# z with time steps on partitions, y gated as it leaves PSUM, q's sums on TensorE, and gates broadcast by DMA

## The chip, the cores and the metric

The kernel runs on one core of a Trainium2 chip. The metric is the device time of one execution in microseconds (us). The engines are TensorE (PE), VectorE (DVE), ScalarE (ACT), GpSimd (POOL) and SyncE (SP, which issues every DMA here). Each executes its own list of instructions in order, and they meet only in semaphores.

## The reference, cut to what matters

Eight sequences of 256 steps and 256 channels pass through a Mamba block and then a linear attention block.

```python
xz = xn @ in_proj_w.T;  x_in, z = split(xz)            # 512 channels each
u  = silu(causal_conv4(x_in) + conv_b)
dt, B, C from x_proj(u)                                # N = 16 states
h  = h * exp(dt * A) + (dt * u) * B                    # scan over 256 steps
y  = sum_n(h * C) + u * D_param
y  = y * silu(z)                                       # gated
x  = x + gate[b] * (y @ out_proj_w.T)                  # gate: one row of 256 per batch
q  = softmax over the 32 channels of a head;  k = softmax over the 256 steps
att = k.T @ v (per head);  y = q @ att
x  = x + (silu(ln(y) * (1 + scale) + shift) @ W_out + b_out)
```

## The kernel before, in words

**Units.** A batch's scan has 512 channels (4 chunks `dc` of 128 partitions) by 16 states. It is cut into 16 units `g`, each of one chunk and 4 states: 128 partitions by 4 x 256 steps. Eight batches give 128 units. For each, ACT computes the decays into one of two PSUM buffers `ring` (`decays`, L504), POOL the inputs into one of five buffers `hs` (`inputs_of`, L383), DVE scans (L635) and multiplies by C (L639), and PE adds the four products into the bank `YT`, by transposing matmuls against the identity (L940), which leaves steps on partitions. `decays(g)` waits until the multiplication of unit g-2 has released its ring buffer.

**Slots.** All other work of a batch is a step with a fixed slot, written out by hand: at loop index g every engine first does its part of unit g and then the steps whose slot, plus 16 times a batch, equals g (`due`). Since slots count modulo 16, three batches are interleaved: the projections of the next (slots -24 to -1), the scan (0 to 15), and what follows the scan (16 to 41). Below, "position" is the slot modulo 16.

**Around y.** After a chunk's four units DVE copies `YT` to `yt` (`copy_sums`, L646, at positions 4, 8, 12 and 0). At slot 18 (position 2) PE waits for the four copies and transposes them back into the banks PZ and PY (`transpose_back`, L956), behind `in_proj_2` of a later batch, which waits for DVE's convolution taps. At slot 19 (position 3) DVE multiplies the two banks by `zs` = silu(z), channels on partitions (`gate_y`, L654), into `yg`, the input of `out_proj` (PE, slot 19). Then come `gate_x` (DVE, slot 21), `residual` (POOL, slot 24) and the attention block.

**Around z.** `in_proj` (PE, L901) has four calls; calls 2 and 3 give z, and ACT copies or gates their result (L451, L455, L457).

**Around q and k.** DVE takes the maxima of q over heads and of k over steps, subtracts q's, and negates k's with a `tensor_scalar` on 128 x 2 elements (`max_qk`, position 11, L673 to L682). ACT exponentiates (`exp_qk`, position 14). DVE sums q's exponentials over heads and takes both reciprocals (`sums_qk`, position 13, L686 to L692). PE multiplies k by v (`k_times_v`, L1016, slot 31) when ACT has copied both transposes; DVE scales the result into `att` (`head_blocks`, L699, position 0); PE multiplies q by it (L1024); DVE divides by q's sums (`normalize_q`, L706, position 1).

**Gates.** During the first batch PE multiplies rows of the identity by `gate8` to spread each batch's gate row over 128 partitions, in two halves (`setup_gates`, L865), and DVE copies the banks PY and PZ to `gate` (L787, g = 11 and 14).

**ACT at position 7** does `silus`: two table loads around the silus of z, u and, from the fourth on, of the attention block's output.

Of the kernel before, what the change touches and what calls it, by code (L numbers as in the profile page):

```python
# [19 lines left out]
P = 128  # L20
# [41 lines left out]
def build(nc, a, out):  # L62
    ctx = ExitStack()
    with ctx:
# [28 lines left out]
        gate = sb("gate", [P, NB, D])  # L93
# [12 lines left out]
        zs = sb("zs", [P, 2, DC, T])  # L106
# [8 lines left out]
        yt = sb("yt", [P, DC, TC, P])  # L115
# [7 lines left out]
        qmax, qsum, rq = sb("qmax", [P, TC, HEADS]), sb("qsum", [P, TC, HEADS]), sb("rq", [P, TC, HEADS])  # L123
# [9 lines left out]
        fin = sb("fin", [P, TC, D])  # L133
        bc_dram = nc.dram_tensor("bc_rows", (2, 2 * N, T), F32, kind="Internal").ap()
# [32 lines left out]
        s_gate_mm = sem("gate_mm")  # L167
        s_gate_ready = sem("gate_ready")
# [30 lines left out]
        s_yt_ready = sem("yt_ready")  # L199
# [22 lines left out]
        s_qrec_step = sem("qrec_step")  # L222
# [21 lines left out]
        bc_loaded = [[sem(f"bc_loaded{i}_{q}") for q in range(UPC)] for i in range(2)]  # L244
        s_out_stored = sem("out_stored")
# [5 lines left out]
        def xz_bank(b, h):  # L251

            return (PX, PY, PZ, ring[:, 0, 0:2, :])[h] if b == 0 else PX

# [7 lines left out]
        def _(sp):  # L262
# [6 lines left out]
            def broadcast_bc(b):  # L269
# [142 lines left out]
        def _(act):  # L412
# [34 lines left out]
            def copy_z(b):  # L447
                act.wait_ge(s_xz_mm, 4 * b + 3)
                if b >= 2:
                    act.wait_ge(s_yg_ready, 2 * (b - 1))  # L450
                nc.scalar.activation(zs[:, b % 2, 0:2, :], xz_bank(b, 2)[:, :, :], ACT.Copy).then_inc(s_z_ready, 1)  # L451

            def silu_z(b):
                act.wait_ge(s_z_ready, 3 * b + 1)
                nc.scalar.activation(zs[:, b % 2, 0:2, :], zs[:, b % 2, 0:2, :], ACT.Silu).then_inc(s_z_ready, 1)  # L455
                act.wait_ge(s_xz_mm, 4 * b + 4)
                nc.scalar.activation(zs[:, b % 2, 2:4, :], xz_bank(b, 3)[:, :, :], ACT.Silu).then_inc(s_z_ready, 1)  # L457
# [49 lines left out]

            def normalize1(b):
# [18 lines left out]
            def exp_qk(b):  # L527
                act.wait_ge(s_qsub_ready, b + 1)
                nc.scalar.activation(qe[:, :, :], qe[:, :, :], ACT.Exp).then_inc(s_qe_ready, 1)
                act.wait_ge(s_kmax_ready, 2 * (b + 1))  # L530
# [50 lines left out]
            for g in range(FIRST, LAST):  # L581
# [6 lines left out]
                for slot, step in ((-17, normalize0), (-16, modulated), (-15, conv_last_tap_0), (-14, conv_last_tap_1),  # L588
                                   (-11, copy_z), (-6, copy_xdbl), (-5, softplus_parts_0), (-3, softplus_parts_1),
                                   (25, normalize1), (26, norm1), (30, exp_qk), (31, mask_v), (32, copy_qT),  # L590
# [9 lines left out]
        def _(dve):  # L600
# [41 lines left out]
            def copy_sums(b, dc):  # L642
# [467 lines left out]
```

## Time and profile before

| | us |
|---|---|
| median of 3 runs | 667.79 |
| lowest, highest | 666.66, 671.83 |
| profiled execution | 668.15 |
| its span, first to last instruction | 666.3 |
| DVE busy | 589.3 |
| PE busy, PE weight loads busy | 452.1, 376.6 |
| ACT busy | 405.9 |
| POOL busy | 389.4 |

The profile records one execution; 1.85 us of its time lie outside the span. Busy time counts an instruction from start to end, and consecutive DVE instructions can overlap by some tens of ns, so distances between starts are the better measure of what an instruction costs. The mean granted TensorE clock was 0.843 of full speed.

### The profile page before, as it was taken

Reading aid. Unit: us, or ns where it says so; the run is one execution under the profiler, and the core shown is the slowest. Engines: PE = TensorE matmul, PEld = TensorE weight load, DVE = VectorE, ACT = ScalarE, POOL = GpSimd, SP = SyncE. Lnnn points to the kernel's source line nnn. Section 1 sums busy time; section 2 is a strip of 40 time slices with the busy share of each in tenths; the row PEclk is TensorE's granted clock in tenths of the full one; section 3 lists DMA queues with packets and bytes.
Section 4 is the critical chain, followed back from the end, with each engine's and each line's share of the span. In section 5 each row is a group of like instructions: output and inputs, shape, how many; then the busy total and the mean of one; then the engine's idle time right before and its main releaser. Section 6 shows DMA issues by size and latency. Waiting matters only on the chain.

```text
span 666.3 us, 7102 instructions
## 1 busy us (share of the span) xinstructions
PE 452.1 (68%) x2352; PEld 376.6 (57%) x2352; DVE 589.3 (88%) x618; ACT 405.9 (61%) x874; POOL 389.4 (58%) x292
## 2 busy tenths in 40 slices
PE   3848687678566756778567856776666956775764
PEld 3637566566465645666456745665665756654642
DVE  4809999999999999999999999999999999999321
ACT  2374756558655868387755866487737774754232
POOL 4066759547855786557845694657746696661100
PEclk9978876898689789889689778989789966877886
DMA  7273042002400070005200160007000240000000
GB/s 214 70 248 122 1 162 92 1 16 78 178 1 0 19 268 1 0 17 179 92 0 13 50 226 1 0 16 260 12 0 1 82 190 0 1 16 1 0 16 17
DMA packets 19870, 44.31 MB, mean 67 GB/s; under 512 B 2348, under 2 KB 11060, under 8 KB 19829
## 3 DMA queue, kind: packets, MB, share of 16 engines
q1 hardware_dynamic: 19832, 43.84, 18.9%
q8 instruction: 19, 0.31, 0.2%
q14 instruction: 19, 0.16, 0.1%
HBM read 41.48 MB, written 2.36 MB: 66 GB/s over the span
## 4 chain that ended last, share of the span: by engine, by line
DVE 58%; issue 14%; PE 11%; ACT 9%; POOL 6%; DMA 1%; DVEq 0%; SPq 0%; ACTq 0%; POOLq 0%
DVE ring L635 33%; DVE hs L639 8%; DVE conv L625 5%; POOL hs L383 4%; PE YT L940 3%; ACT ring L504 3%; PE PY L983 2%; DVE st L605 2%; DVE yt L646 2%; DVE kmax L682 2%; PE PX L901 1%; ACT L455 1%; PE PX L836 1%; PE PY L1024 1%; ACT L578 1%
## 5 line engine op out<-in xcount | busy, mean ns | idle before, releaser
L383 POOL TENSOR_TENSOR hs<-dtu,BC 128x1024 f32<-128x1024 f32 x128 | 299.7, 2358 | 107.8 <-PE YT L940 107.7
L635 DVE TENSOR_TENSOR_SCAN ring<-ring,hs 128x1024 f32<-128x1024 f32 x128 | 292.1, 2282 | 20.2 <-POOL hs L383 16.2
L504 ACT ACTIVATE ring<-dt,Aneg 128x256 f32<-128x256 f32 x512 | 213.2, 464 | 149.2 <-DVE hs L639 149.1
L940 PE MATMUL YT<-ident,hs 128*128 128x128 f32 x1024 | 160.0, 312 | 51.5 <-DVE hs L639 51.4
L940 PEld LDWEIGHTS YT<-ident,hs 128*128 128x128 f32 x1024 | 139.9, 163 | 67.6 <-DVE hs L639 62.5
L639 DVE TENSOR_TENSOR hs<-ring,BC 128x1024 f32<-128x1024 f32 x128 | 156.8, 1225 | 4.4
L901 PE MATMUL PX<-xnT,win 128*128 128x256 f32 x232 | 67.0, 439 | 27.2 <-ACT xnT L435 11.2
L901 PEld LDWEIGHTS PX<-xnT,win 128*128 128x128 f32 x232 | 48.8, 222 | 39.9 <-ACT xnT L435 13.6
L983 PE MATMUL PY<-wqkvo,xT 128*128 128x256 f32 x192 | 63.3, 489 | 0.0
L983 PEld LDWEIGHTS PY<-wqkvo,xT 128*128 128x128 f32 x192 | 49.5, 258 | 10.2
L362 POOL TENSOR_TENSOR dt<-dt,conv 128x512 f32<-128x512 f32 x16 | 20.3, 1271 | 53.0 <-ACT conv L484 53.0
L935 PE MATMUL YT<-ident,uD 128*128 128x128 f32 x64 | 16.4, 347 | 46.3 <-DVE yt L646 44.7
L444 ACT ACTIVATE conv<-PX,par 128x256 f32<-128x256 f32 x30 | 15.2, 557 | 47.2 <-PE PX L901 47.2
L935 PEld LDWEIGHTS YT<-ident,uD 128*128 128x128 f32 x64 | 9.4, 176 | 50.1 <-DVE hs L639 49.7
L625 DVE SCALAR_TENSOR_TENSOR conv<-PX,par,conv 128x255 f32<-128x255 f32 (+2 forms) x90 | 36.3, 473 | 0.8 <-ACT conv L444 0.8
L345 POOL TENSOR_SCALAR ve<-mv 128x2 f32<-128x2 f32 x24 | 5.3, 222 | 53.2 <-DVE mv L608 51.8
L389 POOL TENSOR_TENSOR x<-x,xg 128x512 f32<-128x512 f32 x8 | 10.2, 1276 | 42.9 <-DVE x L663 42.9
L966 PE MATMUL PY<-wo,yg 128*128 128x256 f32 x128 | 29.1, 381 | 1.2 <-DVE yg L654 1.1
L979 PE MATMUL PY<-rows,ones 97*128 97x512 bf16 x24 | 12.1, 504 | 25.9 <-ACT xT L553 23.1
L966 PEld LDWEIGHTS PY<-wo,yg 128*128 128x128 f32 x128 | 24.2, 190 | 4.9 <-DVE yg L654 1.7
L1024 PE MATMUL PY<-att,qT 128*128 128x128 f32 x64 | 13.3, 373 | 13.9 <-DVE att L699 13.9
L365 POOL TENSOR_TENSOR dtu<-dt,u 128x512 f32<-128x512 f32 x16 | 20.3, 1269 | 1.3
(126 smaller groups left out, 601.4 us busy)
## 6 DMA issues: line engine op xcount, KB each, us to landing
BC<-bc_rows SPq DMA_DIRECT2D x32, 1024.0 KB, 10.1
xg<-in_x SPq DMA_DIRECT2D x8, 256.0 KB, 2.8
out<-fin SPq DMA_DIRECT2D x8, 256.0 KB, 12.3
BC<-in_ada_wT SPq DMA_DIRECT2D x3, 512.0 KB, 5.0
win<-in_in_wT SPq DMA_DIRECT2D x2, 512.0 KB, 6.7
BC<-in_W_emb SPq DMA_DIRECT2D x2, 512.0 KB
wo<-in_out_wT SPq DMA_DIRECT2D x1, 512.0 KB, 13.0
bc_rows<-xdbl SPq DMA_DIRECT2D x8, 32.0 KB, 1.5
```

Of the source, the lines that this page charges most:

```text
L362: nc.gpsimd.tensor_tensor(dt[:, b % 2, half], dt[:, b % 2, half], vln[:, half], ALU.add).then_inc(s_dt_sum, 1)
L365: nc.gpsimd.tensor_tensor(dtu[:, b % 2, half], dt[:, b % 2, half], u[:, b % 2, half], ALU.mult).then_inc(s_dtu_ready, 1)
L383: nc.gpsimd.tensor_tensor(hs[:, g % DBUF], dtu[:, b % 2, dc, :].unsqueeze(1).to_broadcast([P, NQ, T]), BC[:, b % 2, NQ * q:NQ * q + NQ, :] ...
L504: ins = nc.scalar.activation(ring[:, g % 2, j, :], dt[:, b % 2, dc, :], ACT.Exp, scale=Aneg[:, c:c + 1])
L625: V.scalar_tensor_tensor(conv[:, dc, s:], xz_bank(b, h)[:, e, 0:T - s], w, conv[:, dc, s:], ALU.mult, ALU.add).then_inc(s_tap_done, 1)
L635: V.tensor_tensor_scan(states, states, driven, 0.0, ALU.mult, ALU.add).then_inc(s_scan_done, 1)
L639: V.tensor_tensor(hs[:, g % DBUF], ring[:, g % 2], BC[:, b % 2, N + NQ * q:N + NQ * q + NQ, :], ALU.mult).then_inc(s_hc_ready, 1)
L901: ins = M(xz_bank(b, h)[:, e, :], win[:, k, lo:lo + P], xnT[:, k, :], start=(k == 0), stop=(k == KD - 1))
L935: ins = M(YT[:, c, :], uD[:, dc % 2, P * c:P * c + P], ident[:, :], is_transpose=True, start=(c == 0), stop=False, skip_group_check=True)
L940: ins = M(YT[:, c, :], hs[:, g % DBUF, j, P * c:P * c + P], ident[:, :], is_transpose=True, start=False, stop=(q == UPC - 1 and j == NQ - ...
L966: ins = M(PY[:, c, :], yg[:, k, P * c:P * c + P], wo[:, k, :], start=(k == 0), stop=(k == DC - 1))
L983: ins = M(dst[:, c, :], xT[:, k, P * c:P * c + P], wqkvo[:, w, k, :], start=False, stop=(k == KD - 1), skip_group_check=True)
```

## The change

z's two projections take 128 steps of the normalized input as the stationary operand and all 512 z weights as the moving one, so z comes out with steps on partitions. DVE's copy of `YT` becomes the gating multiplication, at the same places. The gated sums are transposed back as before, and what DVE did at slot 19 becomes two ACT copies at slot 19. k's maximum is reduced with `negate=True`, the separate negation goes. q's head sums become matmuls of `qT` against four columns of the block mask, into a free part of PZ, ahead of the matmuls of `k_times_v`; their reciprocal is read from PSUM after `att`. The gate rows are written to DRAM and broadcast by DMA, one per batch, two buffers.

```diff
+            def load_gate(b):                                   # SP
+                if b >= 2:
+                    sp.wait_ge(s_gated, b - 1)
+                sp.dma_start(gate[:, b % 2, :], gate_dram[b].unsqueeze(0).to_broadcast([P, D])).then_inc(
+                    gate_loaded[b % 2], 16)
...
             load_x(2)
+            sp.wait_ge(s_gate8_ready, 1)
+            sp.dma_start(gate_dram, gate8[:, :]).then_inc(s_gate_stored, 16)
+            sp.wait_ge(s_gate_stored, 16)
+            load_gate(0)
+            load_gate(1)
...
                 if b + 2 < NB:
                     load_x(b + 2)
+                if b + 1 < NB:
+                    load_gate(b + 1)
...
+            def copy_yg(b):                                     # ACT, slot 19
+                for h, bank in ((0, PZ), (1, PY)):
+                    act.wait_ge(s_yback_mm, 2 * b + h + 1)
+                    if b >= 1:
+                        act.wait_ge(s_out_mm, b)
+                    nc.scalar.activation(yg[:, 2 * h:2 * h + 2, :], bank[:, :, :], ACT.Copy).then_inc(s_yg_ready, 1)
...
-            def copy_sums(b, dc):                               # DVE
+            def gate_y(b, dc):
                 dve.wait_ge(s_y_acc, U * b + UPC * (dc + 1))
+                dve.wait_ge(s_z_ready, 3 * b + 3)
                 if b >= 1:
                     dve.wait_ge(s_yback_mm, 2 * b)
-                V.tensor_copy(yt[:, dc], YT[:, :, :]).then_inc(s_yt_ready, 1)
-            def gate_y(b):
...
+                V.tensor_tensor(ygT[:, :, P * dc:P * dc + P], YT[:, :, :], zs[:, b % 2, :, P * dc:P * dc + P],
+                                ALU.mult).then_inc(s_ygT_ready, 1)
...
-                V.tensor_reduce(kmax[:, :], PZ[:, :, :], AX.X, ALU.max).then_inc(s_kmax_ready, 1)
+                V.tensor_reduce(kmax[:, :], PZ[:, :, :], AX.X, ALU.max, negate=True).then_inc(s_kmax_ready, 1)
...
-                V.tensor_scalar(kmax[:, :], kmax[:, :], -1.0, None, ALU.mult).then_inc(s_kmax_ready, 1)
...
-                V.tensor_reduce(qsum[:, :, :].rearrange("p c h -> p (c h)"), ..., AX.X, ALU.add)
-                V.reciprocal(rq[:, :, :], qsum[:, :, :]).then_inc(s_qrec_step, 1)
...
                     V.scalar_tensor_tensor(att[:, k, :], ...)   # head_blocks
+                V.reciprocal(rq[:, :, :].rearrange("p c h -> p (c h)"), PZ[:, 1, 0:TC * HEADS]).then_inc(s_qrec_ready, 1)
...
-            def gate_rows(half):                                # DVE, and setup_gates on PE
...
+                    c = h - 2                                   # in_proj, calls 2 and 3
+                    for k in range(KD):
+                        ins = M(flat(xz_bank(b, h)), xnT[:, k, P * c:P * c + P], win[:, k, DI:2 * DI], start=(k == 0),
+                                stop=(k == KD - 1))
...
                 pe.wait_ge(s_kT_ready, b + 1)                   # k_times_v
                 pe.wait_ge(s_qT_ready, b + 1)
+                for c in range(TC):
+                    for h in range(KD):
+                        lo = HEADS * c + HEADS // KD * h
+                        M(PZ[:, 1, lo:lo + HEADS // KD], qT[:, h, P * c:P * c + P], blockmask[:, 0::DH], start=True,
+                          stop=True)
```

## Rows read from the trace of the kernel before

**Rows 1.** The page: each engine's busy us, share, instructions; the chain that ended last.
```profile
PE 452.1 (68%) x2352; PEld 376.6 (57%) x2352; DVE 589.3 (88%) x618; ACT 405.9 (61%) x874; POOL 389.4 (58%) x292
...
DVE 58%; issue 14%; PE 11%; ACT 9%; POOL 6%; DMA 1%; DVEq 0%; SPq 0%; ACTq 0%; POOLq 0%
```

**Rows 2.** Groups by line and shape: busy us, mean ns, idle before.
```profile
L646 DVE COPY yt<-YT 128x256 f32<-128x256 f32 x32 | 13.3, 416 | 2.6 <-PE YT L940 2.6
L682 DVE TENSOR_SCALAR kmax<-kmax 128x2 f32<-128x2 f32 x8 | 11.8, 1476 | 0.0
L673 DVE TENSOR_REDUCE qmax<-PY 128x16 f32<-128x512 f32 x8 | 5.5, 682 | 7.1 <-PE PY L983 7.1
L686 DVE TENSOR_REDUCE qsum<-qe 128x16 f32<-128x512 f32 x8 | 5.4, 676 | 0.6 <-ACT qe L529 0.6
L692 DVE RECIPROCAL rq<-qsum 128x16 f32<-128x16 f32 x8 | 2.0, 250 | 0.0
L787 DVE COPY gate<-PY 128x512 f32<-128x512 f32 x2 | 1.4, 681 | 0.0
L543 ACT ACTIVATE qT<-PZ 128x512 f32<-128x512 f32 x8 | 4.7, 586 | 0.5 <-PE PZ L829 0.5
```

**Rows 3.** L682's spread, then timelines of DVE and POOL: start, us, engine, line.
```profile
L682 DVE TENSOR_SCALAR kmax<-kmax x8: 158/1974/1990, 169.8 to 644.3; 128x2 f32<-128x2 f32 x8
169.84 1.99 DVE L682 TENSOR_SCALAR kmax<-kmax 128x2 f32<-128x2 f32 x1
171.74 2.28 DVE L635 TENSOR_TENSOR_SCAN ring<-ring,hs 128x1024 f32<-128x1024 f32 x1
167.14 4.67 POOL L383 TENSOR_TENSOR hs<-dtu,BC 128x1024 f32<-128x1024 f32 x2
```

**Rows 4.** Timelines at position 3 of the second batch: PE, ACT, DVE.
```profile
203.40 1.99 PE L901 MATMUL PX<-xnT,win 128*128 128x256 f32 x8 [1.24 <-DVE conv L625]
205.67 0.60 PE L956 MATMUL PY<-ident,yt 128*128 128x128 f32 x4
200.12 3.26 ACT L504 ACTIVATE ring<-dt,Aneg 128x256 f32<-128x256 f32 x8
206.50 1.22 DVE L639 TENSOR_TENSOR hs<-ring,BC 128x1024 f32<-128x1024 f32 x1
207.65 0.68 DVE L654 TENSOR_TENSOR yg<-PZ,zs 128x512 f32<-128x512 f32 x1
208.84 2.29 DVE L635 TENSOR_TENSOR_SCAN ring<-ring,hs 128x1024 f32<-128x1024 f32 x1
225.19 2.30 DVE L635 TENSOR_TENSOR_SCAN ring<-ring,hs 128x1024 f32<-128x1024 f32 x1 [0.56 <-ACT ring L504]
```

**Rows 5.** Timelines at position 3 of the first batch: PE, DVE.
```profile
131.29 3.78 PE L901 MATMUL PX<-xnT,win 128*128 128x256 f32 x8 [0.37 <-DVE conv L625]
135.72 0.65 PE L956 MATMUL PY<-ident,yt 128*128 128x128 f32 x4
136.03 0.69 DVE L654 TENSOR_TENSOR yg<-PZ,zs 128x512 f32<-128x512 f32 x1 [1.33 <-PE PZ L956]
137.24 2.29 DVE L635 TENSOR_TENSOR_SCAN ring<-ring,hs 128x1024 f32<-128x1024 f32 x1
```

**Rows 6.** Timelines of `k_times_v` and `att`, early, late and after the last scan.
```profile
190.02 1.16 PE L1016 MATMUL PZ<-vm,kT 128*128 128x128 f32 x8 [1.02 <-ACT kT L547]
192.88 0.60 DVE L699 SCALAR_TENSOR_TENSOR att<-PZ,rk,blockmask 128x128 f32<-128x128 f32 x2
552.77 2.08 PE L1016 MATMUL PZ<-vm,kT 128*128 128x128 f32 x8 [1.12 <-ACT kT L547]
554.89 0.61 DVE L699 SCALAR_TENSOR_TENSOR att<-PZ,rk,blockmask 128x128 f32<-128x128 f32 x2 [0.59 <-PE PZ L1016]
618.72 1.92 PE L1016 MATMUL PZ<-vm,kT 128*128 128x128 f32 x8
648.86 1.16 PE L1016 MATMUL PZ<-vm,kT 128*128 128x128 f32 x8 [0.69 <-ACT kT L547]
```

More of the change, by code:

```diff
@@ L92, in build @@
         gate8 = sb("gate8", [NB, D])
-        gate = sb("gate", [P, NB, D])
+        gate = sb("gate", [P, 2, D])
         mods = sb("mods", [P, 4 * KD, NB])
@@ L244, in build @@
         bc_loaded = [[sem(f"bc_loaded{i}_{q}") for q in range(UPC)] for i in range(2)]
+        gate_loaded = [sem(f"gate_loaded{i}") for i in range(2)]
         s_out_stored = sem("out_stored")
@@ L253, in xz_bank, with flat @@
             return (PX, PY, PZ, ring[:, 0, 0:2, :])[h] if b == 0 else PX
+        def flat(bank):
+            return bank.rearrange("p e t -> p (e t)")
         def over_batches(col):
@@ L780, in add_emb_bias @@
                     V.tensor_tensor(m1b[:, k, :], m1b[:, k, :], mods[:, 3 * KD + k, :], ALU.add).then_inc(s_emb_ready, 1)
-            def gate_rows(half):
-                dve.wait_ge(s_gate_mm, half + 1)
-                for i, bank in ((0, PY), (1, PZ)):
-                    b = NB // 2 * half + 2 * i
-                    V.tensor_copy(gate[:, b:b + 2, :], bank[:, :, :]).then_inc(s_gate_ready, 1)
-            def gate_rows_0():
-                gate_rows(0)
-            def gate_rows_1():
-                gate_rows(1)
             def conv_taps_0(b):
@@ L815, in _ @@
                     setup()
-                for at, step in ((3, setup_gate8), (8, add_emb_bias), (11, gate_rows_0), (14, gate_rows_1)):
+                for at, step in ((3, setup_gate8), (8, add_emb_bias)):
                     if g == at:
@@ L854, in setup_emb @@
                 setup_mods(pm, embT, 0).then_inc(s_emb_mm, 1)
-            def setup_gates(half):
-                pe.wait_ge(s_gate8_ready, 1)
-                if half == 0:
-                    pe.wait_ge(s_emb_ready, 1)
-                else:
-                    pe.wait_ge(s_gate_ready, 2)
-                for i in range(NB // 2):
-                    b = NB // 2 * half + i
-                    ins = M((PY, PZ)[i // 2][:, i % 2, :], ident[0:NB, b:b + 1].to_broadcast([NB, P]), gate8[:, :],
-                            start=True, stop=True)
-                ins.then_inc(s_gate_mm, 1)
-            def setup_gates_0():
-                setup_gates(0)
-            def setup_gates_1():
-                setup_gates(1)
             def transpose_x(b):
@@ L897, in in_proj @@
                     pe.wait_ge(s_z_ready, 3 * b + 1)
-                for e in range(2):
-                    lo = P * (2 * h + e)
+                if h < 2:
+                    for e in range(2):
+                        lo = P * (2 * h + e)
+                        for k in range(KD):
+                            ins = M(xz_bank(b, h)[:, e, :], win[:, k, lo:lo + P], xnT[:, k, :], start=(k == 0),
+                                    stop=(k == KD - 1))
+                else:
+                    c = h - 2
                     for k in range(KD):
-                        ins = M(xz_bank(b, h)[:, e, :], win[:, k, lo:lo + P], xnT[:, k, :], start=(k == 0), stop=(k == KD - 1))
+                        ins = M(flat(xz_bank(b, h)), xnT[:, k, P * c:P * c + P], win[:, k, DI:2 * DI], start=(k == 0),
+                                stop=(k == KD - 1))
                 ins.then_inc(s_xz_mm, 1)
@@ L1067, in _ @@
                         step(b)
[L1068 to L1070 removed]
+                if g == 0:
+                    setup_emb()
 def kernel(x, cond_2048, mask_BxSx1_fk1, L0_cond_ln_g, L0_cond_ln_b, L0_cond_ada_w, L0_cond_ada_b, L0_cond_in_proj_w,
```

67 lines of the change are left out of this document (26 added, 41 removed).

## The prediction

> **What bounds the kernel now.** I read the page first: DVE is busy for 589.3 of 666.3 us, and the chain that ended last runs over it for 58% [rows 1]. The groups by line then show DVE's price list and how little of its idle time stands before each group [rows 2]. Between the first scan and the last, DVE is the bound: what leaves it there shortens the kernel, provided that what it waits for next is already there. So the timelines decide, and I read them at the positions that the change touches. There the distance between starts, not the busy time, is what an instruction costs DVE.
>
> **The change, part by part.**
>
> *k's negation.* It handles two elements per partition and takes 1476 ns on average, against 682 for a reduction over 512 [rows 2]. The spread explains it: 158 ns at least, in the tail where POOL is idle, and nearly 2 us in five of the eight. The one at 169.84 ends at 171.83, just after POOL's pair of input products ends at 171.81 [rows 3]. So the instruction is not slow, it waits for POOL. Busy time is 11.8 us; less 0.16 for the tail and 0.09 of overlap for each of seven (169.84 to 171.74 is 1.90, busy 1.99 [rows 3]) that is **11.0 us** of DVE's line. The Trainium skill (SBUF — State Buffer, Who interferes with whom) says that VectorE's two-port modes, which `tensor_scalar` can enter, and GpSimd exclude each other for a whole instruction, and that on trn2 `tensor_reduce` never contends; by that rule the whole 11.0 goes. What no row shows is a negated reduction. Its bounds are 0 and one more pass of 0.68 us, seven times; I take 0, since the plain one is nearest.
>
> *q's sums.* The reduction (676) and the reciprocal (250) leave position 13 [rows 2]. In starts I take 0.59 and 0.17: each less what its start hides under the one before. Seven batches: **5.3 us**. `rk` stays and must not wait longer: its input comes from ACT, whose work there follows DVE's multiplication at position 12 and shifts with it.
>
> *The reciprocal again.* It returns after `att`, from PSUM, in six batches ahead of a scan: 6 x 0.17, **-1.0**. From PSUM and from SBUF the same reduction differs by 6 ns, 682 against 676 [rows 2], so I add nothing. The Trainium skill (VectorE: DVE Perf Modes, The TRN2 errata) charges a PSUM source 62 cycles more, 0.065 us; by that the sum would be 0.4 us smaller.
>
> *Gate rows.* Four copies of 681 ns (two of them in the row, and their twins from PZ) leave the first batch [rows 2]; in starts 0.60 each: **2.4 us**. The stores and broadcasts go to SP ahead of waits for events that come later anyway: batch b+1's gate is asked for when `gate_x(b-1)` is done, while the load of x just ahead of it waited for `residual(b-1)`, which is later still. The store must only land before the second batch's B and C are ready, seven units on. Each broadcast writes 128 KB by its shape, has a batch's time for it, and nothing else on SP is moved: nothing.
>
> *YT copy becomes gating.* 416 ns for 256 elements from PSUM, and 681 for 512 of the multiplication with one PSUM and one SBUF operand [rows 2]: both come to about 1.04 ns per element above the same fixed part. Nothing; the bounds are -0.1 and +0.1 us for each of 32.
>
> *z's projection.* Four pairs of 256 columns become two pairs of 512: the same columns, half the weight loads. Nothing, with bounds of 0.2 us either way per call, at position 2.
>
> *The two gatings at position 3 and their return on ACT.* DVE is freed of 208.84 - 207.65 = 1.19 us per batch. But ACT now copies both banks between `decays` of units 3 and 4, and those copies wait for PE. Before, ACT had both units' decays done by 203.4, long before the scan of unit 4 at 208.84 [rows 4]. After, in the second batch: PE's last transpose ends at 205.67 + 0.60 = 206.27. The second copy, at 0.586 us [rows 2] and about 0.1 to wake or to follow the first, ends at 206.95; four decays, 3.26 / 2 = 1.63, end at 208.6. DVE is free at 206.50 + 1.22 = 207.7. So it **waits about 0.9 us for the ring**, and the scan starts 0.2 earlier than before. All of this hangs on the taps before it and shifts with DVE. In five batches that gains 5 x 0.15 (I keep 0.05 for semaphores) = 0.75. The last of seven has another order on PE, and I give it nothing. In the first, PE's transposes end at 135.72 + 0.65 = 136.37; copy and decays give 138.75 where the scan stood at 137.24 [rows 5]: -1.5. Together **-0.8**. A freed 8 us is thus a loss. Later in the batch `out_proj` starts after two steps that ACT delayed, about 1 us later against DVE, and `gate_x` may wait 0.4 us. That is covered where the scan of unit 8 waited 0.56 us for ACT [rows 4], a wait counted from position 5 and unchanged by this.
>
> *q's sums on PE.* Eight more instructions (four products, each in two passes) with a full weight load of 128 columns. `k_times_v` has eight of the same loads and takes 1.16 to 2.08 us [rows 6]; in pure loads that is 0.9 or 1.7. Early, PE ends at 191.18 and `att` starts at 192.88: 1.7 us of cover [rows 6]. In the batch at 552.77 DVE already waits 0.59, so there it costs **-1.6**. In the tail all is in line: the one at 618.72 and the one at 648.86 cost 1.7 and 0.9; the copies on ACT take the place of DVE's gatings, which stood behind `stats2`, and give back 0.3. The reduction on DVE was hidden behind ACT's exponentials there. Tail: **-2.3**.
>
> **The sum.** 11.0 + 5.3 - 1.0 + 2.4 - 0.8 - 1.6 - 2.3 = 13.0. The profiled execution took 668.15, the median is 667.79, 0.36 less; I take 13.0 from the median: **654.8**. The bounds: negation in the reduction -4.8; gating +-3; z +-1.5; PE's loads +-1.5; the PSUM reciprocal -0.5. Together 648 to 661.
>
> **The rivals.**
>
> *A, position 3 costs more.* In the first batch the projection takes 3.78 us against 1.99, and the transposes end 1.7 us after DVE was free at 136.03 - 1.33 = 134.70 [rows 4, 5]. If PE ran like that in all batches, the ring would come 1.7 us late each time: five more losses, 8 us, 663. Against it: the same call takes 1.99 us in the four batches that follow the second too; its row stands for the five.
>
> *B, DVE's freed time counts in full.* If ACT's copies slipped into its idle time before the ring is needed, 7 x 1.19 + 1.33 would count as well, in place of -0.8: 10.5 us more, **644**. For it: ACT is not a busy engine. Against it: order and PE's end fix the copies.
>
> *C, slower.* The lock passes on: what waited for POOL is DVE's next SBUF operand, now the scan. Then the 11.0 stays. With it, PE must be late at position 3 as in A (-8): 13.0 - 11.0 - 8 = -6, 674. The point from which it decides is a wait for the ring above 1.8 us per batch, once the 11.0 is lost. The scans run beside POOL all the time at an even 2.28 to 2.30, which speaks strongly against the first half.
>
> *D, the negation's wait passes on alone.* 13.0 - 11.0 = 2: 666. The page named above excludes it for one SBUF operand, and so do the even scans.
>
> *E, the gates' DMAs delay SP* and with it a broadcast of B and C: no row of before has POOL waiting for those in the middle, and I price it inside the range.
>
> **How the numbers follow.** Forecast 0.68, A 0.12, B 0.1, D 0.06, C 0.04. 1% is 6.7 us, about what a measurement tells from no change. Below 661.1 lie the forecast, B and a third of A: 0.82, and I say 0.85 since A is mostly partial; within 1%: 0.11; slower: 0.04. The range of eight in ten runs from 647, some way toward B, to 661.5, some way into A.
>
> **What would show it.** L682 gone and the distance from q's subtraction to the next scan 0.60; a new wait of DVE's L635 for ACT at position 3, near 0.9 us in the middle batches and 4 in the first; full batches that repeat about 2.7 us sooner than before; DVE busy near 558 (589.3 less 11.8, 5.4, 16 x 0.68 and 4 x 0.68); a tail, from the last scan's multiplication to the end, 2 us longer. A gain of 4 us per batch means B, one of 1 A or D. The forecast is wrong if a DVE instruction that is now short comes out stretched beside POOL, or if ACT reaches the decays of unit 4 much later than the 3.6 us after the taps' end that I count on (206.95 against 203.34).

## The result, and the profile after

Over 15 runs each on the same chips the kernel after takes 664.75 us (661.07 to 667.69), the one before 668.45 (664.62 to 671.83): a ratio of 0.9949 with an interval of 0.9926 to 0.9973. The gain is 3.7 us where 13.0 were forecast, and 664.75 lies above the range. The profiled execution took 664.89, its span is 663.1 against 666.3, its mean granted clock 0.833 against 0.843. All ratios and their intervals leave out executions more than 1.5% above the fastest of the same kernel. Each kernel has one trace, of one execution; where that execution is not near the kernel's median, the text says so.

The page after, busy time of each engine as in [rows 1]:

```profile
PE 462.5 (70%) x2336; PEld 371.5 (56%) x2336; DVE 561.9 (85%) x582; ACT 412.9 (62%) x890; POOL 389.3 (59%) x292
```

DVE lost 27.4 us of work, the span 3.2. So most of the work went as foreseen (busy near 558 was the forecast, 3.9 below what came) and idle time came in its place. PE is busier by 10.4 us although it has fewer instructions: the first hint that it ran slower. The groups of DVE by line and form, columns as in [rows 2], say where the idle time stands:

```profile
L659 DVE TENSOR_TENSOR_SCAN ring<-ring,hs 128x1024 f32<-128x1024 f32 x128 | 292.1, 2282 | 31.0 <-POOL hs L400 16.2 <-ACT ring L521 14.8
L671 DVE TENSOR_TENSOR ygT<-YT,zs 128x256 f32<-128x256 f32 x32 | 13.3, 414 | 2.4 <-PE YT L925 2.4
L679 DVE TENSOR_TENSOR x<-PY,gate 128x512 f32<-128x512 f32 x8 | 5.5, 690 | 13.2 <-PE PY L953 13.2
L692 DVE TENSOR_REDUCE kmax<-PZ 128x2 f32<-128x512 f32 x8 | 5.5, 681 | 1.9 <-PE PZ L984 1.9
L709 DVE RECIPROCAL rq<-PZ 128x16 f32<-128x16 f32 x8 | 2.0, 245 | 0.0
```

Two new waits: the scan for ACT's decays, 14.8 us (4.0 before), and `gate_x` for `out_proj`, 13.2 us, of which 8.4 are a single one in the tail. The prices of the new instructions are as assumed: gating costs what the copy did (414 against 416 ns), the negated reduction what the plain one did (681), the reciprocal from PSUM what the one from SBUF did (245 against 250).

The clearest view of where time went is the start of each of the 128 scans, after against before: what the difference grows by between two scans is given under the position of the second scan, one behind the steps that stand between them (so the negation, in the steps of position 11, counts under 12). These are sums over the batches, in us, each rounded by itself:

| stretch | after − before | forecast |
|---|---|---|
| up to the first scan | −0.4 | 0 |
| position 12: negation | −11.0 | −11.0 |
| position 14: q's sums | −5.4 | −5.3 |
| reciprocal back | +0.8 | +1.0 |
| gate rows, first batch | −2.4 | −2.4 |
| positions 4, 6, 8: +3.6, +5.4, −2.0 | +6.9 | +0.8 |
| position 1, once, at 117 us | +1.3 | 0 |
| four small waits less (positions 3 and 9) | −1.7 | 0 |
| position 2, 0.06 in each batch | −0.3 | 0 |
| `att` after q's products, late batch | +1.9 | +1.6 |
| tail, last scan's start to the end | +7.0 | +2.3 |
| span | −3.2 | −13.0 |

The loop from first to last scan went from 564.67 to 554.85 us, the tail from 52.9 to 59.9. Two lines of the table carry the error.

**What went right.** DVE's timeline behind the reduction to `kmax`, start, us, engine, line:

```profile
169.56 0.68 DVE L694 TENSOR_TENSOR qe<-PY,qmax 128x512 f32<-128x512 f32 x1
170.15 2.29 DVE L659 TENSOR_TENSOR_SCAN ring<-ring,hs 128x1024 f32<-128x1024 f32 x1
```

The scan starts 0.59 us after q's subtraction, where the negation of [rows 3] stood 1.90 us in between, and the scan is not stretched: the wait for POOL did not move to it.

**Position 3 and 4.** PE, ACT and DVE in the second batch, as in [rows 4]:

```profile
201.15 1.98 PE L885 MATMUL PX<-win,xnT 128*128 128x512 f32 x4 [1.25 <-DVE conv L649]
203.41 0.60 PE L943 MATMUL PY<-ident,ygT 128*128 128x128 f32 x4
204.10 0.59 ACT L530 ACTIVATE yg<-PY 128x512 f32<-128x512 f32 x1
204.58 3.26 ACT L521 ACTIVATE ring<-dt,Aneg 128x256 f32<-128x256 f32 x8
206.29 2.30 DVE L659 TENSOR_TENSOR_SCAN ring<-ring,hs 128x1024 f32<-128x1024 f32 x1 [0.80 <-ACT ring L521]
```

That is the forecast to a tenth: transposes, copy, four decays, a wait of 0.80 (0.9 said). But in the fifth batch:

```profile
414.13 3.64 PE L885 MATMUL PX<-win,xnT 128*128 128x512 f32 x4 [1.24 <-DVE conv L649]
...
418.78 0.59 ACT L530 ACTIVATE yg<-PY 128x512 f32<-128x512 f32 x1
419.26 3.25 ACT L521 ACTIVATE ring<-dt,Aneg 128x256 f32<-128x256 f32 x8
420.96 2.30 DVE L659 TENSOR_TENSOR_SCAN ring<-ring,hs 128x1024 f32<-128x1024 f32 x1 [2.50 <-ACT ring L521]
```

The same four instructions on PE take 3.64 us, everything behind them is 1.7 us later, and the scan waits 2.50. The windows before and in the projection of both batches give the reason; columns are the stretch, its length, busy us (and instructions) of PE, its weight loads, DVE, ACT and POOL, then the granted clock of PE, DMA share and GB/s:

```profile
201.00:204.00 3.00, 2.85 (x12) 1.62 (x12) 2.96 (x6) 0.39 (x1) 1.62 (x5) 1.00 0.00 0
...
407.00:414.00 7.00, 4.70 (x31) 3.97 (x29) 6.96 (x11) 2.58 (x6) 4.73 (x2) 0.97 0.00 0
414.00:418.00 4.00, 3.87 (x8) 1.69 (x9) 3.93 (x7) 0.00 (x0) 2.57 (x5) 0.57 0.02 4
```

In the fifth batch PE fell to little above its lower level (1.2 of 2.4 GHz) for the projection, after seven microseconds near full clock. Over the batches the projection takes 2.57, 1.98, 3.57, 1.98, 3.64 and 3.65 us, and the waits for the ring are 2.31, 0.80, 2.38, 0.80, 2.50, 2.50 and, in the last of the seven, 1.48. The kernel before had 3.78 once and 1.99 five times. Against the kernel before, the stretch to the scan of unit 4 changed by −0.23, −0.31, +1.27, −0.31, +1.39, +1.38 and +0.37 us. The first of these is luck: the forecast took 3.78 us for that projection too and charged 1.5 us, and it came at 2.57.

**`gate_x`.** DVE meets a second wait two positions on. `out_proj` stands on PE behind the last call of `in_proj`, and that call waits until ACT's `copy_z`, of another batch, has freed PX; ACT now does `copy_z` after its two copies and eight decays. PE and DVE in the first batch, then in the fifth:

```profile
137.63 3.62 PE L885 MATMUL PX<-win,xnT 128*128 128x512 f32 x4 [3.28 <-ACT zs L468]
144.80 0.69 DVE L679 TENSOR_TENSOR x<-PY,gate 128x512 f32<-128x512 f32 x1 [1.94 <-PE PY L953]
...
423.08 1.98 PE L885 MATMUL PX<-win,xnT 128*128 128x512 f32 x4 [3.47 <-ACT zs L468]
428.56 0.69 DVE L679 TENSOR_TENSOR x<-PY,gate 128x512 f32<-128x512 f32 x1 [0.24 <-PE PY L953]
```

The forecast had 0.4 us here, covered by a wait at position 8. In four of the six batches it was 0.34 between starts, and that was covered, in the fifth and sixth too, whose projection at position 2 was slow. In the first and the third it was 2.03: there the last call of `in_proj` and `out_proj` together took 7.35 and 7.34 us where the others took 5.60. So what is not covered (+5.4 against −2.0) comes from two batches in which PE ran low in this second place. The kernels b_neg, yundo and b_q below, without y's part, have such a batch once each (2.3 to 2.4 us).

**The tail.** PE and DVE after the last scan, against [rows 6]:

```profile
607.73 0.95 PE L1005 MATMUL PZ<-blockmask,qT 128*128 128x4 f32 x8
608.54 1.75 PE L1009 MATMUL PZ<-vm,kT 128*128 128x128 f32 x8
611.00 2.08 PE L1017 MATMUL PY<-att,qT 128*128 128x128 f32 x8 [0.70 <-DVE att L707]
616.58 6.64 PE L953 MATMUL PY<-wo,yg 128*128 128x256 f32 x16 [0.69 <-ACT yg L530]
...
623.26 0.69 DVE L679 TENSOR_TENSOR x<-PY,gate 128x512 f32<-128x512 f32 x1 [8.38 <-PE PY L953]
```

q's products themselves cost 0.95 and 1.05 us, 2.0 together where 2.6 were forecast. What costs is behind them: `att`'s product takes 2.08 twice where before it took 1.16 twice, the transposes back 2.1 together in place of 1.2, and `out_proj` 6.64 in place of 3.72. The sum, 1.8 for the products' line (0.95 + 1.05, less 0.2 in `k_times_v`) + 1.8 + 0.9 + 2.9 − 0.4 for the copies on ACT, is the 7.0. The windows of the same stretch, columns as above:

```profile
606.00:612.00 6.00, 4.50 (x28) 4.21 (x29) 1.94 (x5) 0.00 (x0) 0.00 (x0) 0.74 0.01 3
612.00:616.00 4.00, 3.01 (x14) 2.34 (x12) 1.69 (x5) 0.67 (x2) 0.88 (x2) 0.50 0.00 0
616.00:623.00 7.00, 6.42 (x16) 5.19 (x17) 0.00 (x0) 2.90 (x4) 0.47 (x3) 0.53 0.00 0
```

And of the kernel before:

```profile
622.00:634.00 12.00, 7.84 (x42) 6.16 (x40) 5.25 (x13) 4.68 (x6) 3.82 (x9) 1.00 0.00 0
```

Same work, half the clock.

### The profile page after: what moved, and what is told of

The parts are those of the page before. It is cut to its first block and busy times, and to the rows that moved or that the text cites. A ratio compares the mean times of both kernels' runs of the same rounds, so it can differ in the third digit from the quotient of the medians.

```text
span 663.1 us, 7068 instructions
## 1 busy us (share of the span) xinstructions
PE 462.5 (70%) x2336; PEld 371.5 (56%) x2336; DVE 561.9 (85%) x582; ACT 412.9 (62%) x890; POOL 389.3 (59%) x292
## 5 line engine op out<-in xcount | busy, mean ns | idle before, releaser
L925 PE MATMUL YT<-ident,hs 128*128 128x128 f32 x1024 | 156.5, 307 | 49.7 <-DVE hs L663 49.6
L925 PEld LDWEIGHTS YT<-ident,hs 128*128 128x128 f32 x1024 | 136.7, 160 | 65.3 <-DVE hs L663 60.6
L970 PE MATMUL PY<-wqkvo,xT 128*128 128x256 f32 x192 | 61.3, 477 | 0.0
L885 PE MATMUL PX<-win,xnT 128*128 128x512 f32 x56 | 35.7, 771 | 24.5 <-ACT zs L468 17.8
L379 POOL TENSOR_TENSOR dt<-dt,conv 128x512 f32<-128x512 f32 x16 | 20.4, 1272 | 54.2 <-ACT conv L501 54.2
L880 PE MATMUL PX<-xnT,win 128*128 128x256 f32 x120 | 36.4, 456 | 9.3 <-ACT xnT L452 8.4
L880 PEld LDWEIGHTS PX<-xnT,win 128*128 128x128 f32 x120 | 26.3, 231 | 16.2 <-ACT xnT L452 10.7
L530 ACT ACTIVATE yg<-PZ 128x512 f32<-128x512 f32 x8 | 4.8, 598 | 47.6 <-PE PZ L943 47.6
L953 PE MATMUL PY<-wo,yg 128*128 128x256 f32 x128 | 33.2, 418 | 0.7 <-ACT yg L530 0.7
L953 PEld LDWEIGHTS PY<-wo,yg 128*128 128x128 f32 x128 | 27.4, 216 | 9.0 <-issue 3.9
L885 PEld LDWEIGHTS PX<-win,xnT 128*128 128x128 f32 x56 | 11.6, 229 | 37.1 <-ACT zs L468 19.4
```

What stands on the lines that cost most here:

```text
L379: nc.gpsimd.tensor_tensor(dt[:, b % 2, half], dt[:, b % 2, half], vln[:, half], ALU.add).then_inc(s_dt_sum, 1)
L880: ins = M(xz_bank(b, h)[:, e, :], win[:, k, lo:lo + P], xnT[:, k, :], start=(k == 0), stop=(k == KD - 1))
L885: ins = M(flat(xz_bank(b, h)), xnT[:, k, P * c:P * c + P], win[:, k, DI:2 * DI], start=(k == 0), stop=(k == KD - 1))
L925: ins = M(YT[:, c, :], hs[:, g % DBUF, j, P * c:P * c + P], ident[:, :], is_transpose=True, start=False, stop=(q == UPC - 1 and j == NQ - ...
L953: ins = M(PY[:, c, :], yg[:, k, P * c:P * c + P], wo[:, k, :], start=(k == 0), stop=(k == DC - 1))
L970: ins = M(dst[:, c, :], xT[:, k, P * c:P * c + P], wqkvo[:, w, k, :], start=False, stop=(k == KD - 1), skip_group_check=True)
```

## The experiments

Questions: what did each part save or cost alone; is the place of ACT's copies the cause of the +6.9; does the new shape of z's products pull the clock down, or q's four-column products, or neither? "Loop" and "tail" are as in the table (before: 564.7 and 52.9; after: 554.9 and 59.9), from the profiled execution; ratios are to the kernel before on the same chip, whose medians were 668.06, 666.22 and 669.1 in the three sets. All kernels compute the whole function.

### First set

**b_neg: before, with the negation alone.**

```diff
-                V.tensor_reduce(kmax[:, :], PZ[:, :, :], AX.X, ALU.max).then_inc(s_kmax_ready, 1)
+                V.tensor_reduce(kmax[:, :], PZ[:, :, :], AX.X, ALU.max, negate=True).then_inc(s_kmax_ready, 1)
...
-                V.tensor_scalar(kmax[:, :], kmax[:, :], -1.0, None, ALU.mult).then_inc(s_kmax_ready, 1)
```

> The kernel before with one edit: k's maximum is reduced with negate=True and the separate negation goes. Theory 1 (the forecast's term is right, and what is missing was lost at position 3 and in the tail): DVE's starts close up by 1.90 us in five batches, 0.51 and 1.06 in the two others, and nothing takes it back: 11.0 us less, 657.4 where the kernel before takes 668.4. Rival 2 (any time freed on DVE runs into PE and ACT): the batches shrink by 1.90 at position 12 and grow again before the next one, and less than 5 us are left, 663.5 or more.

661.04 us, ratio 0.9898 (0.985 to 0.9946); span 656.0, loop 555.4, tail 52.5. The profiled execution gains 10.3, the median 7.0: of six executions three lie at 657.2 to 657.8 and three at 664.3 to 665.2, so a 7 us step from one execution to the next exists without any of the other parts. The traced execution is one of the quick three. In it 11.0 us go at position 12, and 2.4 come back at position 6 of the third batch, where the last call of `in_proj` takes 3.78 us and `out_proj` 4.84. The median lies between the two theories, 657.4 and 663.5. By the medians the smallest edit of the change gains about as much as the whole change or more (the intervals overlap).

**a_yg20: after, with ACT's two copies one slot later,** behind the decays of unit 4.

```diff
-                                   (19, copy_yg), (25, normalize1), ...
-                                   (-11, copy_z), ...
+                                   (20, copy_yg), (-11, copy_z), ...
```

> The changed kernel with ACT's two copies of the gated y one position later (slot 20), behind the decays of unit 4. Theory 1: DVE's waits for the ring at position 4 (2.31, 0.80, 2.38, 0.80, 2.50, 2.50 and 1.48 us, 12.8 together) go, and gate_x, which hangs on out_proj, takes about half of them back: 6 to 8 us less than the changed kernel, 657 to 659. Rival 2 (PE's projection and transposes set the end of that stretch, whatever ACT does): the wait only moves to gate_x two units later, and the time stays at 663 to 665.

654.75 us, ratio 0.9796 (0.9765 to 0.9827); loop 546.6, tail 58.8. One number moved: ten microseconds, more than the 6 to 8 expected. ACT and DVE in the second batch:

```profile
204.32 0.59 ACT L530 ACTIVATE yg<-PY 128x512 f32<-128x512 f32 x1
205.73 1.67 ACT L521 ACTIVATE ring<-dt,Aneg 128x256 f32<-128x256 f32 x4 [0.82 <-DVE hs L663]
...
204.47 1.23 DVE L663 TENSOR_TENSOR hs<-ring,BC 128x1024 f32<-128x1024 f32 x1
205.61 2.29 DVE L659 TENSOR_TENSOR_SCAN ring<-ring,hs 128x1024 f32<-128x1024 f32 x1
```

The decays of unit 4 are done before the copies, the scan starts without a wait, and ACT waits for DVE again instead. Position 4 is now 1.20 us shorter than before in each of six batches and 2.62 in the first, 9.8 together: the whole of DVE's freed gatings, for which rival B had 9.7. But position 6 grew, by 9.2 over the batches against the kernel before: DVE waits for `out_proj` in six batches, longest in the second:

```profile
216.43 0.69 DVE L679 TENSOR_TENSOR x<-PY,gate 128x512 f32<-128x512 f32 x1 [3.47 <-PE PY L953]
```

On PE, the last call of `in_proj` stood ahead of it, released late by ACT's `copy_z` and slow:

```profile
207.97 3.78 PE L885 MATMUL PX<-win,xnT 128*128 128x512 f32 x4 [1.12 <-ACT zs L468]
211.54 4.84 PE L953 MATMUL PY<-wo,yg 128*128 128x256 f32 x16
```

**a_qdve: after, with q's sums back on DVE,** and no products of q against the mask.

```diff
+                V.tensor_reduce(qsum[...], qe[...], AX.X, ALU.add).then_inc(s_qrec_step, 1)
...
-                        M(PZ[:, 1, lo:lo + HEADS // KD], qT[:, h, P * c:P * c + P], blockmask[:, 0::DH], start=True,
-                          stop=True)
```

> The changed kernel with q's head sums back on DVE (reduction and reciprocal at position 13, no products in k_times_v). If each term is what the comparison of the traces says: 0.64 us of DVE per batch come back (4.5), and the 1.87 at att in the last full batch, 0.9 in the tail and the lower granted clock behind those stretches go (up to 4): between 664 and 667. If the lower clock in the tail comes from these products, the tail shrinks by 5 or more and the time is below 663.

662.48 us, ratio 0.9921 (0.989 to 0.9952); loop 559.3, tail 53.1, `out_proj` in the tail 3.72. The loop gives back 4.4 us and the tail returns 6.8. This part as made is worth nothing that can be told from the noise: what it takes from DVE it gives back at the end. In this trace the projection takes 3.60 us in one of the five batches behind the first, and 1.98 in four.

**a_z256: after, with z in products of 256 columns,** same operands, same order.

```diff
+                    for e in range(2):
                         for k in range(KD):
-                            ins = M(flat(xz_bank(b, h)), xnT[:, k, P * c:P * c + P], win[:, k, DI:2 * DI], ...)
+                            ins = M(xz_bank(b, h)[:, e, :], xnT[:, k, P * c:P * c + P],
+                                    win[:, k, DI + T * e:DI + T * e + T], ...)
```

> The changed kernel with z's projection in products of 256 columns instead of 512: same columns, twice the weight loads, as before the change. If the shape is what brought the lower granted clock into the projection at position 2 (3.6 us in place of 2.0 in three of the batches), that call takes 1.99 us in all batches but the first, the waits of 2.4 to 2.5 us at position 4 fall to 0.8, and the time falls by 4 to 6, to 659 to 661. If the clock follows what PE did before (idle stretches), some batches still show 3.5 us or more and the time stays within 2 us of the changed kernel.

664.27 us, ratio 0.9931 (0.9903 to 0.9958), as after; the shape is not the cause. The projection stays slow, in all batches but one this time, and even that took 2.55 (3.78, 2.55, 3.78, 3.36, 3.37, 3.38), here the last:

```profile
486.84 3.38 PE L886 MATMUL PX<-win,xnT 128*128 128x256 f32 x8 [1.24 <-DVE conv L649]
```

One thing was not expected: in the profiled execution the tail took 53.6 us, with q's products in place. This execution was not a usual one: it took 659.51 us, another took 660.04, and the other eight lie at 662.6 to 669.4. Its loop is 1.1 us longer than after's, so all that it gains on the kernel after lies in the tail. In its tail the low level came only behind q's second set of products:

```profile
641.23 2.08 PE L1018 MATMUL PY<-att,qT 128*128 128x128 f32 x8 [0.70 <-DVE att L707]
```

### Second set

**yundo: after, without the y and z part** (negation, q's sums and gates as after; z, `copy_sums` and the gatings on DVE as before).

```diff
-            def gate_y(b, dc):        # and copy_yg on ACT, z with steps on partitions
+            def copy_sums(b, dc):     # and gate_y(b) on DVE at slot 19, z with channels on partitions
```

> The changed kernel without its y part: z is projected with channels on partitions, DVE copies YT and gates at slot 19 as before; the negated maximum, q's sums on PE and the gates by DMA stay. Theory 1 (the y part is what costs): negation 7 to 10 less, gates 2.4 less, q's sums 4.5 less on DVE and 2.8 more at att and in the tail: 11 to 14 less than before, 654 to 657. Rival 2 (the q products or the DMAs cost, or any relief of DVE is taken back): 661 to 665, as the changed kernel.

654.58 us, ratio 0.9832 (0.9781 to 0.9882); span 652.9, loop 549.9. The three parts without the fourth give 11.6 us in the median. The loop is 14.7 us shorter, against 11.0 + 5.3 − 1.0 + 2.4 − 1.6 = 16.1 forecast for these parts. Position 4 is back at the times of before, and position 6 too but for one batch (+2.4, with `out_proj` at 4.86). The tail was 53.0, again quick with q's products in it. The six lie at 652.3 to 660.1, and the traced execution took 654.69.

**y_only: the y and z part and the gates, without the other two.**

```diff
+                V.tensor_scalar(kmax[:, :], kmax[:, :], -1.0, None, ALU.mult).then_inc(s_kmax_ready, 1)
...
+                V.tensor_reduce(qsum[...], qe[...], AX.X, ALU.add).then_inc(s_qrec_step, 1)
...
-                        M(PZ[:, 1, lo:lo + HEADS // KD], qT[...], blockmask[:, 0::DH], start=True, stop=True)
```

> The changed kernel with the separate negation and q's sums on DVE put back: the y and z part and the gates by DMA alone. Theory 1: the two parts that are gone saved 11.0 and 4.5 of DVE's line; what is left are the gates (-2.4) and the y part, whose position 3 to 6 costs about 7: 2 to 6 us more than before, 670 to 674. Rival 2 (the y part is neutral and the loss belongs to its meeting with a shorter DVE line): 664 to 667.

671.82 us over twelve, of which seven lie at 666.9 to 672.9 (median 668.54) and five at 677.2 to 682.1; ratio of the seven 1.0032 (0.9998 to 1.0066); loop 566.5, tail 50.7. The loop got 1.8 longer although the gates save 2.4, so y's part costs 4.2 there and its tail is 2.2 shorter. The kernel a_qdve, with the same y part, has no such gain in the tail (53.1), so I don't count it.

**a_yg20_z4: a_yg20, with `copy_z` one slot earlier,** right behind ACT's copies at position 4.

```diff
-                                   (20, copy_yg), (-11, copy_z), ...
+                                   (20, copy_yg), (-12, copy_z), ...
```

> The changed kernel with ACT's copies of the gated y at slot 20 and ACT's copy of z at slot -12 instead of -11, so ahead of the decays of unit 5. PE's second z projection, out_proj and gate_x then start about 1.7 us earlier against DVE. Theory 1: the waits of gate_x at position 5 (0.6 to 3.5 us) fall below 0.3 in the batches in which PE has its full clock; the wait of unit 8 for the ring, counted from unit 5, returns 0.5 of them in each: 1 to 4 us less than with slot 20 alone, 651 to 654. Rival 2 (PE's clock there falls with the new idle stretch): no gain, 654 to 656.

651.67 us, ratio 0.977 (0.9735 to 0.9806); loop 539.2, tail 61.3. ACT, PE and DVE in the fourth batch:

```profile
340.90 0.60 ACT L468 ACTIVATE zs<-PX 128x512 f32<-128x512 f32 x1
...
342.79 1.88 PE L885 MATMUL PX<-win,xnT 128*128 128x512 f32 x4
344.51 3.62 PE L953 MATMUL PY<-wo,yg 128*128 128x256 f32 x16
...
348.98 0.68 DVE L679 TENSOR_TENSOR x<-PY,gate 128x512 f32<-128x512 f32 x1
```

`copy_z` no longer stands behind unit 5's decays, the last call of `in_proj` and `out_proj` run on PE one after the other, and `gate_x` waits for nothing, here and in four more batches of the loop (0.39 and 0.19 us in the first two). The loop gained another 7.4 us. So with ACT's order mended neither half of the +6.9 is left, though the projection at position 2 still takes 3.78, 3.78 and 3.56 us in the first three batches: the order decides whether a slow projection reaches DVE. What is left is the tail.

**a_yg20_z4_qdve: the same, with q's sums on DVE** (the edits of a_yg20_z4 and a_qdve).

> The kernel with the copies at slots 20 and -12, and q's head sums back on DVE. By the starts, DVE's line gets 0.64 us per batch longer (4.5) and the products' 1.87 at att and 0.9 in the tail go: 1 to 2 us slower than its neighbour, 652 to 656. If the longer tail of the changed kernel (59.9 us from the last scan's start against 52.9) follows the products, the tail falls to 53 and the time to 650 or below.

645.96 us, ratio 0.969 (0.9654 to 0.9725); loop 544.4, tail 52.0. With the order mended, q's sums on PE cost 9.3 us in the tail to save 5.2 in the loop.

### Third set

**a_q64: after, with q's products against 64 columns of the mask instead of four,** the reciprocal reading every sixteenth.

```diff
-                        M(PZ[:, 1, lo:lo + HEADS // KD], qT[:, h, P * c:P * c + P], blockmask[:, 0::DH], start=True,
+                        M(PZ[:, 1, lo:lo + P // 2], qT[:, h, P * c:P * c + P], blockmask[:, 0::2], start=True,
...
-                V.reciprocal(rq[...], PZ[:, 1, 0:TC * HEADS]).then_inc(s_qrec_ready, 1)
+                V.reciprocal(rq[...], PZ[:, 1, 0:T:DH // 2]).then_inc(s_qrec_ready, 1)
```

> The changed kernel with each of q's sum products against 64 columns of the block mask instead of 4 (the reciprocal picks the same 16 sums out of 256 columns). The weight loads, which set the pace of these eight instructions, are the same. If the narrow products are what leaves TensorE at 1.2 GHz behind them, the first out_proj after the last scan takes 3.7 us instead of 6.6 and the tail falls from 59.9 to 54 or less: 658 to 660 in place of 664. If it is the order or the length of the waits around them, the tail stays within 2 us of 59.9 and the time within 2 us of the changed kernel.

Six runs at 660.2, 660.7, 664.6, 676.2, 676.5 and 678.4 us: the time says little (0.9888, 0.9826 to 0.9949, from the lower three, and the upper three are slower than any of the kernel after). The trace, of the one at 660.7, says more. PE in the tail:

```profile
610.80 1.00 PE L1005 MATMUL PZ<-blockmask,qT 128*128 128x64 f32 x8
...
613.46 1.16 PE L1017 MATMUL PY<-att,qT 128*128 128x128 f32 x8 [0.70 <-DVE att L707]
...
617.29 3.72 PE L953 MATMUL PY<-wo,yg 128*128 128x256 f32 x16 [0.74 <-ACT yg L530]
```

And the windows over them:

```profile
611.00:615.00 4.00, 2.91 (x24) 2.53 (x22) 1.54 (x5) 0.00 (x0) 0.00 (x0) 1.00 0.00 0
617.00:621.00 4.00, 3.71 (x18) 3.25 (x19) 0.00 (x0) 2.62 (x4) 1.01 (x3) 1.00 0.00 0
```

Sixteen times the columns take 1.00 us in place of 0.95, the clock stays at 1.00, and the tail is 52.6 us. Taken alone this doesn't single out the width, since a_z256's trace has four columns, nearly the same loop and a tail of 53.6. The next pair does more.

**a_yg20_z4_q64: a_yg20_z4 with the same 64 columns.**

> The same edit on the kernel with the copies at slots 20 and -12, whose tail is 61.3 us. Narrow products as the cause: tail 54 or less, 644 to 646, below the 646.0 of q's sums on DVE. Otherwise 650 to 653.

645.22 us, ratio 0.9629 (0.9588 to 0.9669); loop 539.4, tail 54.2 against 61.3 with four columns. Nothing else differs between the two but what the reciprocal reads, the loops are equal (539.2 and 539.4), and 6.5 us of the median go with it; the two were measured in different sets, but their executions don't overlap (649.6 to 653.2 and 642.7 to 645.4). PE in the tail:

```profile
594.61 1.81 PE L1005 MATMUL PZ<-blockmask,qT 128*128 128x64 f32 x8
...
598.15 1.16 PE L1017 MATMUL PY<-att,qT 128*128 128x128 f32 x8 [0.70 <-DVE att L707]
```

Here the products began at the low clock (1.81 us for the eight), and `att` ran at the full one.

**b_q: before, with q's sums on PE and nothing else** (the four-column products, the reciprocal from PSUM, no reduction).

> The kernel before with q's head sums moved to PE and nothing else: DVE gains 0.64 us in seven batches (4.5), loses 1.9 at att in the sixth, and the tail gets 0.9 longer: 1 to 2 us less than before. If the products bring the lower clock into the tail whatever stands around them, the tail grows by 5 to 9 and the time is 4 us or more above before.

672.0 us over twelve, ratio 1.0045 (1.0014 to 1.0077): 2.9 us slower than before, less than the 4 or more that the second theory wanted. The traced execution, at 674.74, is one of the slower ones: loop 562.4 (2.3 shorter), tail 61.5 (8.6 longer). PE in the tail, and the windows:

```profile
616.78 1.70 PE L1013 MATMUL PZ<-blockmask,qT 128*128 128x4 f32 x8
618.34 2.05 PE L1017 MATMUL PZ<-vm,kT 128*128 128x128 f32 x8
621.10 2.08 PE L1025 MATMUL PY<-att,qT 128*128 128x128 f32 x8 [0.70 <-DVE att L693]
```

```profile
616.00:622.00 6.00, 5.30 (x25) 5.00 (x24) 1.20 (x4) 0.00 (x0) 0.00 (x0) 0.50 0.00 0
...
626.00:633.00 7.00, 6.22 (x16) 5.03 (x17) 0.69 (x1) 2.37 (x3) 0.57 (x3) 0.55 0.01 1
```

In the kernel before, `k_times_v` began at the low clock too (1.92 us, [rows 6]) and the clock was 1.00 from `att` on. Here it begins as low, and stays there far into `out_proj` (6.42 us). The projection at position 2 took 3.78 and 3.58 us in two of the five batches behind the first.

**best_mix: a_yg20_z4 with q's sums on PE in the first five batches and on DVE in the last three.** The gain in the loop is kept where it is covered, and the late `att` and the tail are spared.

```diff
+QPE = 5
+                if b >= QPE:
+                    V.tensor_reduce(qsum[...], qe[...], AX.X, ALU.add).then_inc(s_qsum_step, 1)
...
+                if b < QPE:
+                    for c in range(TC):
...
```

> The kernel with the copies at slots 20 and -12, and q's head sums on PE for the first five batches, on DVE for the last three. For the five, 0.64 us of DVE each (3.2) are gained and the products lie in PE's wait for att; the sixth batch's 1.87 at att and the tail's 0.9 are not paid, and the tail is 52 us as with q's sums on DVE throughout: 642 to 644, the fastest. If the narrow products cost TensorE's clock in the full batches too, 645 to 648.

639.99 us (639.53 to 641.54), ratio 0.9563 (0.9524 to 0.9602); loop 539.1, tail 50.7: the quickest of all, 29 us below before, and 2 to 4 below what was expected. Its page, and its waits of DVE (line waited for, us in total, times, longest):

```profile
PE 448.8 (70%) x2312; PEld 362.8 (57%) x2312; DVE 562.9 (88%) x585; ACT 413.1 (65%) x890; POOL 388.0 (61%) x292
```

```profile
DVE ring L661 <- ACT ring L523: 4.5, 7, 1.2
```

DVE is as busy as in the kernel after, within 1 us, in 25 us less of span. Of the waits for the ring 4.5 us are left of 14.8.

## Why the prediction was wrong

**The prices were right.** Negation 11.0 us, as forecast, with the bound on a negated reduction at its lower end (681 ns); q's reduction 5.4 against 5.3; the reciprocal 0.8 against 1.0; the gate rows 2.4 as said; the gating in place of the copy, nothing; the late `att` 1.9 against 1.6; nothing on SP. The Trainium skill (SBUF — State Buffer, Who interferes with whom) agrees with [rows 3] and with b_neg: without the instruction that ended with POOL's pair, 1.90 us are gone at that place in each of five batches, and no neighbour took them over. The other page named (VectorE: DVE Perf Modes, The TRN2 errata) would make the reduction from PSUM and the reciprocal from PSUM 0.065 us dearer than from SBUF. Neither shows it: 681 ns from PSUM against 676 from SBUF for a reduction over 512, 245 against 250 for the reciprocal.

**The step that failed first is position 3.** The prediction put it as "waits about 0.9 us for the ring", with "the same call takes 1.99 us in the four batches that follow the second too; its row stands for the five". The chain of events was right, and where the clock was full the wait came out at 0.80. But 1.99 was what the kernel before showed, at full clock; it was carried over as if it belonged to the instruction. After, three of six batches had 3.57 to 3.65. Rival A had this mechanism with its condition ("if PE ran like that in all batches") and its price, 663; it was put at 0.12 on the ground of those rows of before. It held in three batches of the six.

**The second half of that step is `gate_x`.** "`gate_x` may wait 0.4 us. That is covered" was right wherever the clock was full or fell at position 2 alone: 0.34 in four batches. It had no case for a low clock in what stands ahead of `gate_x` on PE, the last call of `in_proj`, released late by ACT's `copy_z`, and `out_proj`. In two batches that cost 2.03 us each. Together positions 4 to 8 cost 6.9 where 0.8 was in the sum: 6.1 of the 9.8 us by which the span fell short, and the cheap first batch hides another 1.7. a_yg20 and a_yg20_z4 show what made DVE pay: the same instructions one slot on give 8.2 and then 7.4 us of the loop.

**The third is the tail.** The term counted q's products as eight more instructions at the loads' price, 1.7 + 0.9. They cost 0.95 and 1.05. What was not in it is that the work behind them can run at half the clock: 2.9 us in `out_proj`, 0.9 in each product with `att`, 0.9 in the transposes. The tail took 4.7 us more than forecast. The trace of b_q shows it with nothing else changed, and a_yg20_z4_q64 shows it gone with the narrow shape; a_yg20_z4_qdve, without the products, gains 9.3 us in the tail.

**The rest**: 1.3 us at position 1 once, at 117 us, where DVE waits 1.18 us for PE's sums behind a projection of 3.78 us (as long in the kernel before, where DVE, with two gate rows more to copy, came later and didn't wait), against 1.7 us of small waits that were absorbed. B was wrong for the kernel as it stands, and right for the scan's own wait in a_yg20, where its freed 1.20 per batch appears to the digit. C and D are excluded by the even scans. E is excluded by the table: no stretch is left for it.

**What stays open.** Why the clock is lower in z's projection is not settled. It is not the width of z's products (a_z256). Of the five batches behind the first, those with 3.2 us or more in that call number none in before and b_neg; one in yundo and two in b_q, with q's products and without y's part; one in a_qdve and one in y_only, with y's part and without q's products; and with both three in after, four in a_z256 and a_q64. With ACT's order moved they number one to four, with q's products on PE or without. So either part may have a share, but this is one execution of each kernel, and the counts settle nothing. That the gatings' 1.2 us per batch, moved from DVE to ACT, shift the rhythm of PE's bursts is a guess that no run tests. Nor is each execution the same: b_neg's six split into two groups 7 us apart.

## What to carry over

When a step goes into an in-order queue that also feeds a double buffer, put it behind the next unit's work and not ahead of it, and follow what the steps further down the same queue release; here one slot was worth ten microseconds of 665, more than most of the change's arithmetic. A duration of a TensorE group read before a change is a reading at one clock level: take the sum at both levels wherever the change moves what stands around it, and give that case a chance to match. And judge a part that helps the loop by the tail too: a choice by batch (best_mix) kept one and dropped the other.

## What the runs showed of the hardware

Eight fp32 products with four moving columns each, in line ahead of dependent work, can be followed by a low granted clock for most of that work. Of the six kernels traced with four-column products in the last two batches, four (after, b_q, a_yg20, a_yg20_z4) ran the first `att` product after the last scan in 2.08 us and `out_proj` in 5.9 to 6.6, with tails of 58.8 to 61.5 us. Two (yundo, a_z256) ran them in 1.16 and 3.72, and a_z256 was traced in an execution quicker than eight of its ten, so four to two is a count of executions more than of kernels. Of the eight without, by 64 columns or by a sum on DVE, all eight had 1.16 and 3.72 and tails of 50.7 to 54.2. In yundo and a_z256 the eight products took 0.95 us, so PE was at full clock when they began, and it kept it; in b_q and a_yg20_z4 they took 1.70 and 1.71, the low level, and it stayed low (in a_yg20 1.39, between the two). In the kernel after they took 0.95 and the clock was low from `k_times_v` on. So narrow products don't always have a low clock behind them. But where it was low in this place, it came back only while `out_proj` ran, and not ahead of `att` as it did behind wide ones in a_yg20_z4_q64 and with none in the kernel before. This is shown for the tail alone: inside the loop `att`'s product took 1.9 us or more in every kernel, with narrow products or without, in one to five of the five early batches (five in after, two in before). Widening them costs 0.05 us at full clock.

A TensorE group at the same place can also change its level between batches of one execution, with the same instructions ahead of it (1.98 and 3.64 us for z's projection). And an instruction on two elements per partition can cost 1.9 us on DVE's line beside GpSimd and 0.16 without (the negation in the kernel before).
